# A wavelet convolution's raw vectors, laid out with the taps innermost and read with a stride by GpSimd

## The reference, cut to what matters

```python
for i in range(3):                       # Haar levels
    co = haar2d(cur); cur = co[:, :, 0]
    flat = dwconv(co.reshape(B, C * 4, h, w), wconv_w[i]) * wscale[i]   # 5x5 for each channel
    level_coeffs.append(flat.reshape(B, C, 4, h, w))
for i in reversed(range(3)):
    next_ll = ihaar2d(level_coeffs[i].at[:, :, 0].add(next_ll))
x = x + dwconv(gn_x, base_w) * base_scale + base_b + next_ll
```

## Time and profile before

| | us |
|---|---|
| median of 3 runs | 11089.34 (11088.98 to 11091.86) |
| the profiled execution | 11089.43 |
| its span, first to last instruction | 11087.6 |
| TensorE busy | 10521.8 (95%) |
| VectorE busy | 9222.0 (83%) |
| ScalarE busy | 7175.4 (65%) |
| GpSimd busy | 3609.4 (33%) |

### The profile page before, as it was taken

How to read it: one execution, slowest core, us unless ns; L and a number is a source line. 1 busy time by engine, 2 the same in 40 slices (tenths; PEclk the granted TensorE clock), 3 DMA queues, 4 the chain that set the end, 5 groups by cost and what they waited for, 6 DMA issues and landing times. The chain is left out here.

```text
span 11087.6 us, 205333 instructions
## 1 busy us (share of the span) xinstructions
PE 10521.8 (95%) x66084; PEld 8954.3 (81%) x66084; DVE 9222.0 (83%) x16479; ACT 7175.4 (65%) x11852; POOL 3609.4 (33%) x3715
## 2 busy tenths in 40 slices
PE   4999999999999999999969999999999999999999
PEld 4888888888888888888758888888888888888887
DVE  6999989899998999988867777777777777777777
ACT  4777777777777777778745555555555555555554
POOL 3444444444443444444322222222222222222222
PEclk9999999999999999999989999999999999999999
DMA  5333333233333323322267777777777777777775
GB/s 185 132 99 119 110 107 133 85 133 95 122 120 98 120 97 125 114 81 80 63 129 156 156 153 154 155 154 153 152 155 155 156 154 153 155 154 153 152 153 124
DMA packets 1162861, 1453.43 MB, mean 131 GB/s; under 512 B 215391, under 2 KB 1125023, under 8 KB 1125279
## 3 DMA queue, kind: packets, MB, share of 16 engines
q1 hardware_dynamic: 1161055, 1442.80, 51.5%
q10 hardware_dynamic: 1376, 6.13, 0.1%
HBM read 1040.11 MB, written 408.56 MB: 131 GB/s over the span
## 5 line engine op out<-in xcount | busy, mean ns | idle before, releaser
L1438 DVE SCALAR_TENSOR_TENSOR ob<-ps_w,prm,x 64x512 f32<-64x512 f32 x1920 | 1440.4, 750 | 1048.9 <-PE ps_w L1346 1010.1
L1292 PE MATMUL ps_w<-zb,mat 128*128 128x512 f32 x4800 | 1927.2, 401 | 107.4 <-DVE ob L1438 107.4
L1294 PE MATMUL ps_w<-zb,mat 128*128 128x512 f32 x4800 | 1907.7, 397 | 0.0
L1293 PE MATMUL ps_w<-zb,mat 128*128 128x512 f32 x4800 | 1907.6, 397 | 0.0
L634 POOL CAST xn_hi<-xs 96x512 fp32r<-96x512 f32 x1024 | 843.0, 823 | 3107.5 <-PE ps_qkv L659 2253.1
L1243 ACT ACTIVATE z<-x,prm 64x384 f32<-64x384 f32 (+1 forms) x3072 | 1815.9, 662 | 58.8 <-DVE x L1369 51.0
L1185 POOL CAST mat<-raw 128x1280 fp32r<-128x1280 f32 (+1 forms) x288 | 393.8, 1385 | 4048.4 <-DMA raw<-vec 2318.0
L657 PE MATMUL ps_qkv<-wqkv_hi,xn_hi 96*128 96x288 f32 x4096 | 1388.4, 339 | 37.3 <-POOL xn_lo L636 19.9
L636 POOL TENSOR_TENSOR xn_lo<-xs,xn_hi 96x512 fp32r<-96x512 f32 x1024 | 1365.0, 1333 | 82.2
L1292 PEld LDWEIGHTS ps_w<-zb,mat 128*128 128x128 f32 x4800 | 904.0, 188 | 402.4 <-DVE ob L1438 184.6
L658 PE MATMUL ps_qkv<-wqkv_lo,xn_hi 96*128 96x288 f32 x4096 | 1212.8, 296 | 0.0
(11 more groups left out here) (196 smaller groups left out, 23299.6 us busy)
## 6 DMA issues: line engine op xcount, KB each, us to landing
xst<-in_x SPq DMA_DIRECT2D x96, 2048.0 KB, 13.8
xs<-in_x SPq DMA_DIRECT2D x128, 1536.0 KB, 8.9
y_scratch<-ys SPq DMA_DIRECT2D x128, 1536.0 KB, 9.5
out<-ob SPq DMA_DIRECT2D x768, 208.0 KB
xb<-in_x SPq DMA_DIRECT2D x576, 256.0 KB
yb<-y_scratch SPq DMA_DIRECT2D x576, 256.0 KB
raw<-vec SPq DMA_DIRECT2D x192, 320.0 KB, 4.2
raw<-vec SPq DMA_DIRECT2D x384, 160.0 KB, 3.9
```

The source lines that it names most:

```text
L1292: mm(out_, w[HI], xx[HI], start=start, stop=False)
L1293: mm(out_, w[HI], xx[LO], start=False, stop=False)
L1294: return mm(out_, w[LO], xx[HI], start=False, stop=stop)
L1438: last = v.scalar_tensor_tensor(out=ob[p:p + WROWS, t // 2].rearrange("p b w -> p (b w)")[:, q::2], in0=ps_w[t][q * WROWS:(q + 1) * WROWS, ...
```

## The change

`pads`, the three DRAM vectors and the raw tiles are laid out with the taps innermost: element n of all ten tap vectors, then element n+1. raw1 becomes [128, 64, 10], raw2 and raw3 [128, 128, 10]. Each partition's part of raw is then one run in DRAM and in SBUF (640 or 1280 elements, 2560 or 5120 B), and each of the ten DMAs has one run for each partition. The matrices keep their layout, and the number and the sizes of GpSimd's casts and subtractions are the same, but their read of raw has a step of ten elements (40 B), backwards. The first stage's copies into `pads` write with other strides; those from `full1` no longer transpose what they read.

```diff
-                p1 = pad1.rearrange("p (ia q dj o n) -> p ia q dj o n", ia=2, q=2, dj=TAPS, o=2)
+                p1 = pad1.rearrange("p (ia q n dj o) -> p ia q n dj o", ia=2, q=2, dj=TAPS, o=2)
...
-                                o = 1 - p
+                                o = p
                                 first = WROWS - 3 - oa
-                                full = p1[:, ia, q, :, o, first:first + 2 * TAPS - 1:2]
-                                link(g.tensor_copy(full, full1[:, (ia + oa) % 2, (q + p) % 2].rearrange("p di dj -> p dj di")))
+                                full = p1[:, ia, q, first:first + 2 * TAPS - 1:2, :, o]
+                                link(g.tensor_copy(full, full1[:, (ia + oa) % 2, (q + p) % 2]))
...
-                p2 = pad2.rearrange("p (ia ab dj n) -> p ia ab dj n", ia=2, ab=2, dj=TAPS)
-                p3 = pad3.rearrange("p (ia ab dj n) -> p ia ab dj n", ia=2, ab=2, dj=TAPS)
+                p2 = pad2.rearrange("p (ia n ab dj) -> p ia n ab dj", ia=2, ab=2, dj=TAPS)
+                p3 = pad3.rearrange("p (ia n ab dj) -> p ia n ab dj", ia=2, ab=2, dj=TAPS)
...
-            raw1 = sb_("raw1", [128, 2 * TAPS, WROWS])
-            raw2 = sb_("raw2", [128, 2 * TAPS, HALF])
-            raw3 = sb_("raw3", [128, 2 * TAPS, HALF])
+            raw1 = sb_("raw1", [128, WROWS, 2 * TAPS])
+            raw2 = sb_("raw2", [128, HALF, 2 * TAPS])
+            raw3 = sb_("raw3", [128, HALF, 2 * TAPS])
...
-                        sp.dma_start(raw2[ia:128:2, :, :],
-                                     bass.AP(tensor=vec2.tensor, offset=c * (NV2 * V2) + (ia * 2 * TAPS * V2 + 2),
-                                             ap=[[2, HALF // 2], [V2, 2 * TAPS], [1, HALF]])).then_inc(raw_in, 16)
+                        sp.dma_start(raw2[ia:128:2].rearrange("p n t -> p (n t)"),
+                                     bass.AP(tensor=vec2.tensor, offset=c * (NV2 * V2) + (ia * V2 + 2) * (2 * TAPS),
+                                             ap=[[2 * (2 * TAPS), HALF // 2], [1, HALF * 2 * TAPS]])).then_inc(raw_in, 16)
...
                 def build(turned, hi_done, ready, count):
-                    for mat, raw, form in turned:
-                        last = nc.gpsimd.tensor_copy(mat[HI][:].rearrange(form), raw)
+                    for mat, raw, form, m_ in turned:
+                        last = nc.gpsimd.tensor_copy(mat[HI][:].rearrange(form, m=m_), raw)
...
-                        lo, hi = mat[LO][:].rearrange(form), mat[HI][:].bitcast(F32).rearrange(form)
-                        for d in range(0, raw.shape[1], 2):
-                            at = slice(d, min(d + 2, raw.shape[1]))
+                        lo, hi = mat[LO][:].rearrange(form, m=m_), mat[HI][:].bitcast(F32).rearrange(form, m=m_)
+                        taps = 2 * HALF // raw.shape[2]
+                        for d in range(0, raw.shape[1], taps):
+                            at = slice(d, min(d + taps, raw.shape[1]))
                             last = nc.gpsimd.tensor_tensor(lo[:, at], raw[:, at], hi[:, at], ALU.subtract)
...
-                        build([(mat1[k], raw1[:].rearrange("p (d o) m -> p d (o m)", o=2)[:, :, ::-1], "p d m -> p d m")],
+                        build([(mat1[k], raw1[:].rearrange("p m (d o) -> p (d o) m", o=2)[:, :, ::-1],
+                                "p d (o m) -> p (d o) m", WROWS)],
...
-                        build([(mat2, raw2[:, :, ::-1], "p s d m -> p (s d) m"),
-                               (mat3, raw3[:, :, ::-1], "p s d m -> p (s d) m")],
+                        build([(mat2, raw2[:].rearrange("p m t -> p t m")[:, :, ::-1], "p s d m -> p (s d) m", HALF),
+                               (mat3, raw3[:].rearrange("p m t -> p t m")[:, :, ::-1], "p s d m -> p (s d) m", HALF)],
```

More of the change, by code:

```diff
@@ L322, in _ @@
                                     lo = first + 2 * dis[0]
-                                    part = p1[:, ia, q, dj, o, lo:lo + 2 * len(dis) - 1:2]
+                                    part = p1[:, ia, q, lo:lo + 2 * len(dis) - 1:2, dj, o]
                                     link(g.tensor_tensor(part, part, base_t[:, r_:r_ + 2 * len(dis) - 1:2, c_ + 2 * n],
                                                          ALU.add))
-                p2 = pad2.rearrange("p (ia ab dj n) -> p ia ab dj n", ia=2, ab=2, dj=TAPS)
-                p3 = pad3.rearrange("p (ia ab dj n) -> p ia ab dj n", ia=2, ab=2, dj=TAPS)
+                p2 = pad2.rearrange("p (ia n ab dj) -> p ia n ab dj", ia=2, ab=2, dj=TAPS)
+                p3 = pad3.rearrange("p (ia n ab dj) -> p ia n ab dj", ia=2, ab=2, dj=TAPS)
                 for ia in range(2):
@@ L330, in _ @@
                         for oa in range(2):
-                            t2 = sum_t[:, 1, ab, (ia + oa) % 2, :].rearrange("p (di dj) -> p dj di", dj=TAPS)
+                            t2 = sum_t[:, 1, ab, (ia + oa) % 2, :].rearrange("p (di dj) -> p di dj", dj=TAPS)
                             first = HALF - 3 - oa
-                            link(g.tensor_copy(p2[:, ia, ab, :, first:first + 2 * TAPS - 1:2], t2))
+                            link(g.tensor_copy(p2[:, ia, first:first + 2 * TAPS - 1:2, ab, :], t2))
                         for rho in range(4):
-                            t3 = sum_t[:, 2, ab, (ia + rho // 2) % 2, :].rearrange("p (di dj) -> p dj di", dj=TAPS)
+                            t3 = sum_t[:, 2, ab, (ia + rho // 2) % 2, :].rearrange("p (di dj) -> p di dj", dj=TAPS)
                             first = HALF - 5 - rho
-                            link(g.tensor_copy(p3[:, ia, ab, :, first:first + 4 * TAPS - 3:4], t3))
+                            link(g.tensor_copy(p3[:, ia, first:first + 4 * TAPS - 3:4, ab, :], t3))
                 pool.sem_inc(padded, 1)
@@ L1110, in load_raw @@
                             first = q * WROWS + ia
-                            sp.dma_start(raw1[first:first + WROWS - 1:2, :, :],
+                            sp.dma_start(raw1[first:first + WROWS - 1:2].rearrange("p n t -> p (n t)"),
                                          bass.AP(tensor=vec1.tensor,
-                                                 offset=c * (NV1 * V1) + ((2 * ia + q) * 2 * TAPS * V1 + 2),
-                                                 ap=[[2, WROWS // 2], [V1, 2 * TAPS], [1, WROWS]])).then_inc(raw_in, 16)
+                                                 offset=c * (NV1 * V1) + ((2 * ia + q) * V1 + 2) * (2 * TAPS),
+                                                 ap=[[2 * (2 * TAPS), WROWS // 2], [1, WROWS * 2 * TAPS]])).then_inc(raw_in, 16)
                     for ia in range(2):
-                        sp.dma_start(raw2[ia:128:2, :, :],
-                                     bass.AP(tensor=vec2.tensor, offset=c * (NV2 * V2) + (ia * 2 * TAPS * V2 + 2),
-                                             ap=[[2, HALF // 2], [V2, 2 * TAPS], [1, HALF]])).then_inc(raw_in, 16)
+                        sp.dma_start(raw2[ia:128:2].rearrange("p n t -> p (n t)"),
+                                     bass.AP(tensor=vec2.tensor, offset=c * (NV2 * V2) + (ia * V2 + 2) * (2 * TAPS),
+                                             ap=[[2 * (2 * TAPS), HALF // 2], [1, HALF * 2 * TAPS]])).then_inc(raw_in, 16)
                     for rho in range(4):
-                        sp.dma_start(raw3[rho:128:4, :, :],
+                        sp.dma_start(raw3[rho:128:4].rearrange("p n t -> p (n t)"),
                                      bass.AP(tensor=vec3.tensor,
-                                             offset=c * (NV2 * V2) + (rho // 2 * 2 * TAPS * V2 + 4),
-                                             ap=[[4, HALF // 4], [V2, 2 * TAPS], [1, HALF]])).then_inc(raw_in, 16)
+                                             offset=c * (NV2 * V2) + (rho // 2 * V2 + 4) * (2 * TAPS),
+                                             ap=[[4 * (2 * TAPS), HALF // 4], [1, HALF * 2 * TAPS]])).then_inc(raw_in, 16)
                 def load(c, g):
```

## The result

| | median, us | lowest to highest | ratio to before |
|---|---|---|---|
| before, on the same chip | 11089.16 | 11088.78 to 11091.86 (4 runs) | |
| after | 11154.69 | 11152.43 to 11161.3 (4 runs) | 1.0059 (95% interval 1.0047 to 1.0072) |

The change costs 65.5 us. The forecast was 11138 us, the range 11080 to 11380. Profiled, the span went from 11087.6 to 11151.8 us, +64.2.

The account below looks back on a forecast made before the run. TensorE was taken to bound the kernel, reached by GpSimd only through VectorE's blocked instructions before the up-sampling. 11089.4 us plus 52 for stalls less 3 for DMA at the start gave 11138 us, range 11080 to 11380.

Parts of the forecast that it names:

- DMA in the loop, 0: Raw loads in the loop: longer runs shorten a landing for which only GpSimd waits, so 0 us.
- At the start: Stage's start, ten serial DMA issues before the first x loads: -3 us, bounds -7 and 0.
- The cast's price, 0.83 ns an element: GpSimd's strided read of raw: 0.83 ns more per element, so a cast of 1280 gets 1.06 us longer.
- The subtraction's price, 0.21 us: GpSimd's subtraction of 256, one of two inputs strided: 0.21 us longer, at the same price per element.
- The chain's growth: VectorE's instructions up to L1426, waiting out GpSimd's casts and subtractions: +2.70 or +2.91 us by channel parity.
- pattern A: One channel parity, 48 of 96 channels: L1426 has 2.51 us to spare before the up-sampling; B, the other, 2.02.
- The stalls: TensorE before the up-sampling: waits of 0.19 and 0.89 us by channel parity, 48 channels each, 52 us.
- mat3's need, SP's wait: covered: Build's end, 4.3 us later at 8023.5: before TensorE needs mat3 (6 us left) and before SP's wait, so no cost.
- Window 1: covered: VectorE's make_in loses about 0.7 us to the build; window 1's copy-out still ends before TensorE wants it, no cost.
- the read below 0.62 ns: Rival at GpSimd's strided read: the slack hides all of it, 11081 to 11092 us, likeliest 11087; chance 0.33.
- the one at twice the price: Rival at GpSimd's strided read: 1.67 ns an element, window 1's copy-out late too, 11503 us; chance 0.18.
- the DMA side: Rival at the loads: fewer runs land the first loads earlier or thin the traffic, 11060 us; chance 0.05.

Follow-up runs that it names:

- dma_only: The changed kernel with its new vectors and DMAs, but casts and subtractions reading raw neighbour by neighbour: 11089.69 us, ratio 1.0.
- halves: The changed kernel with each cast of 1280 elements cut into two of 640: 11129.16 us, ratio 1.0039.
- late_build: The changed kernel, with GpSimd starting mat2 and mat3 only after VectorE's chain has issued its last instruction: 11183.76 us, ratio 1.01.
- dose2: The kernel before with two more casts of 1280 neighbours in each build of mat2 and mat3: 11087.97 us, ratio 0.9999.
- up_first_after: The changed kernel with TensorE doing window 0's up-sampling matmul before sum_down instead of behind it: 11261.12 us, ratio 1.0157.

## Why the prediction was right, point by point

- *The size*: the forecast was 49 us over the kernel before, the measurement is 65.5. That it came out as a loss at all hung on one choice: the rows gave 0.6 to 1.0 ns an element for the strided read, and at 0.62 and below the prediction's own sum gives nothing. The middle of that band was close to the truth, and the errors of the other terms partly cancel, as the points below show.
- *What bounds it, and the path of the loss*: as forecast. TensorE waits at the up-sampling's weight load for VectorE's chain, in both parities; groups without a build are unchanged (L1411 0.41 us at 8066.27).
- *DMA in the loop, 0*: shown by dma_only. *At the start, -3 us within -7 to 0*: sized too high. The loop starts 1.3 us earlier, but 1.1 us of that is there before the first raw issue (5584.98 against 5586.08). From that issue to the loop's start it is 82.8 us instead of 83.0. The ten issues take 6.2 instead of 6.7 us and the raw bytes are the same.
- *The pads, 0*: right; vec1 is sent at 58.68 us instead of 59.84. The copies that now read neighbours went from 0.219 and 0.228 to 0.207 and 0.204 us. 0.204 is the line of the neighbour casts, which fits the reading that the excess on which the price was built was the strided read. It isn't shown, since the same edit changed the steps of their writes.
- *The cast's price, 0.83 ns an element*: measured 0.91 (2.41 us alone against 1.25), in the first build. Sized 9% low.

```profile
5600.18 2.41 POOL L1185 CAST mat<-raw 128x1280 fp32r<-128x1280 f32 x1
5602.77 0.86 POOL L1194 TENSOR_TENSOR mat<-raw,mat 128x256 fp32r<-128x256 f32 x1 [0.18 <-POOL mat L1185]
```

- *The subtraction's price, 0.21 us*: measured 0.13 (0.86 against 0.73). Sized too high: the price of the cast was taken over to an instruction that takes longer for each element anyway, and no row supported that.
- *The chain's growth*: forecast +2.70 us in pattern A and +2.91 in B. Over the middle 88 channels the traces give 9.85 to 12.81 (+2.96) and 10.35 to 13.39 (+3.04). With the measured prices the prediction's own sum would give 2x1.16+2x0.13-0.30+0.13 = +2.41 in A and +2.54 in B (-0.30 where it had -0.06, since shorter subtractions end earlier), so the subtraction's error outweighs the cast's, and 0.5 us is missing. 0.4 of it is a term that the prediction left out, GpSimd's own waits: VectorE's instructions hold up each cast by 0.98 and 0.69 us now (3.38 and 3.09 against 2.40), where it was 0.78 and 0.47 (2.03 and 1.72 against 1.25). Why a blocked strided cast loses 0.2 us more than a blocked one of neighbours no run here settles.
- *The stalls*: forecast 0.19 and 0.89 us, 52 us; the start of the up-sampling moved by 0.45 and 1.04 us, 72 us, of which 0.12 us a channel (12 us) come back at window 0's copy-out. That leaves 60 of the loop's 65.4 us; the next point has the rest.
- *mat3's need, SP's wait: covered*: no such wait shows. *Window 1: covered*: wrong in pattern A. The copy-out is waited for 42 times more and 17 us longer in all (201.4 against 184.6), and all 42 are waits for window 1. `make_in` loses about 1 us there (in the build shown L1394's pair takes 1.76 us where it takes 0.75), not 0.7, and that is the whole cover. The prediction had named such a wait as the sign of a price above 1.1 ns; it shows at 0.91, so the sign was set wrong. halves and late_build show what lies behind it.
- *Two slips in the sums*, without consequence: mat1's build would grow by 1.06 us with the prediction's prices, to 3.7 us and not 4.1, and at 1.1 ns the sum gives stalls of 1.3 and 2.1 us and about 11250 us, not 11230.
- *The rivals*: the read below 0.62 ns and the one at twice the price both fall by the casts' rows (0.91 ns), and dma_only excludes the DMA side.
- *The Trainium skill* (GPSIMD Engine Reference, "Performance pitfalls for Q7 kernels") had half as much again for a step over 8 bytes, and 11148 us by it. The total agrees within 0.1%, the terms don't: the cast at 40 B takes 93 to 96% more, the subtraction 18 to 20% more, and a step of 12 B is the one that costs the cast half as much again. The measurement decides; the page's total came out because the two errors cancel.

## What to carry to other kernels

An engine that is a third busy and waits for its input can still set the end, through another engine that has to wait its instructions out. Before a GpSimd instruction is made longer, look for VectorE's instructions with two SBUF inputs that start while it runs, and for how much the last of them has to spare before TensorE wants it. What counts there is the length of the single GpSimd instruction in the way and where the whole block ends, so cut long ones, and keep the block clear of both neighbouring chains. When TensorE has to wait, look at the granted clock too: waits of up to 2.0 us cost only themselves here, some of those of about 3 us cost clock besides. Fewer and longer DMA runs gave nothing here, because nobody who sets the end waited for the landing.

## What the runs showed of the hardware

- GpSimd's cast of fp32 pays for the step of its read up to 16 B, and no more up to 48 B (each measured once): 1280 elements 1.25, 1.32, 1.89, 2.46, 2.47, 2.48, 2.45 and 2.40 us for steps of 4, 8, 12, 16, 20, 32, 40 and 48 B, and backwards the same as forwards (1.25 and 2.44).
- Its subtraction hides most of that: 0.72, 0.73, 0.84 and 0.87 us over 256 elements for 4, 8, 16 and 40 B.
- VectorE's instructions with two SBUF inputs and GpSimd's alternate one by one: in dose2 four casts in a row delay four VectorE instructions by one cast each. VectorE's with one input in PSUM take their 0.42 us beside GpSimd (L1417).
- The wait goes both ways: a cast of neighbours takes 1.72 to 2.03 us instead of 1.25 beside VectorE's chain, a strided one 3.09 to 3.38 instead of 2.40.
- TensorE's granted clock stayed at 2.4 GHz in loops whose longest waits were 1.1 us (the changed kernel) and 2.0 us (late_build), and fell to 1.2 GHz 33 times about the end of the 95 waits of 2.7 to 3.4 us in up_first_after.
